# A four-layer transformer trunk on one core: the tiles and copies of two attentions in another order

## The reference, cut to what matters

```python
def _mha(x, y, wq, wk, wv, li1_w, li1_b, ..., causal):
    xn = _ln(x, lnx_g, lnx_b)
    yn = _ln(y, lny_g, lny_b)
    q = jnp.einsum('bsc,hcd->bhsd', xn, wq)
    k = jnp.einsum('btc,hcd->bhtd', yn, wk)
    v = jnp.einsum('btc,hcd->bhtd', yn, wv)
    a = jax.nn.softmax(jnp.einsum('bhsd,bhtd->bhst', q, k) * D ** (-0.5), axis=-1)
    if causal:
        a = a * mask                      # after the softmax
    o = jnp.einsum('bhst,bhtd->bhsd', a, v)
    o = o.transpose(0, 2, 1, 3).reshape(x.shape[0], x.shape[1], H * D)
    x_out = x + o @ li1_w + li1_b
    ...
x = _ln(xx, ln1_g, ln1_b)
x = x + _mha(x, x, a1_..., causal=True)    # stage L2a1, 128 keys
x = _ln(x, ln2_g, ln2_b)
return x + _mha(x, ee, a2_..., causal=False)   # stage L2a2, 77 keys of the context
```

## Time and profile before

| | |
|---|---|
| median of 3 runs | 1132.48 us |
| lowest and highest | 1130.48 and 1135.90 us |
| the profiled execution | 1135.39 us |
| its span in the trace | 1133.7 us |
| L2a1 in the trace, from its first table load to its last product | 450.1 to 602.3 us |
| L2a2, the same | 631.6 to 764.1 us |

### The profile page before, as it was taken

The page is one execution under the profiler, slowest core; times in us unless marked ns, Lnnn a source line. Parts: engine busy times, 40 slices in busy tenths (PEclk is TensorE's granted clock), DMA queues, the critical chain, the costliest instruction groups (busy, mean ns, idle before and its releaser), DMA issues. The chain is left out here.

```text
span 1133.7 us, 35842 instructions
## 1 busy us (share of the span) xinstructions
PE 870.2 (77%) x14276; PEld 670.3 (59%) x14340; DVE 831.6 (73%) x2248; ACT 701.4 (62%) x1469; POOL 570.7 (50%) x600
## 2 busy tenths in 40 slices
PE   3788678779998565688888688989569966876776
PEld 2466477547677354255675466775468944655675
DVE  4888767788877897688877777757566767887555
ACT  4887467766665665676558666657156755974444
POOL 3575735665557345264363422222542656867375
PEclk9898779989999977799999899988679977996588
DMA  5363143411110100100001000000033230111120
GB/s 138 91 136 49 47 123 104 101 41 38 30 30 21 45 12 30 46 22 13 4 4 48 2 3 4 4 4 1 29 96 107 76 80 24 56 34 53 48 73 21
DMA packets 63584, 53.48 MB, mean 47 GB/s; under 512 B 14480, under 2 KB 51859, under 8 KB 63293
## 3 DMA queue, kind: packets, MB, share of 16 engines
q1 hardware_dynamic: 57196, 41.95, 13.9%
q0 software_dynamic: 4544, 8.43, 2.5%
q10 hardware_dynamic: 1683, 0.81, 0.3%
HBM read 34.53 MB, written 17.24 MB: 46 GB/s over the span
## 5 line engine op out<-in xcount | busy, mean ns | idle before, releaser
L1501 ACT ACTIVATE area<-psum 128x512 bf16<-128x512 f32 (+2 forms) x164 | 85.7, 538 | 114.3 <-PE psum L786 54.1
L2137 DVE TENSOR_TENSOR area<-psum,area 128x512 bf16<-128x512 f32 (+3 forms) x156 | 92.6, 618 | 36.6 <-ACT area L1501 34.9
L2843 DVE TENSOR_TENSOR area<-area 128x512 bf16<-128x512 f32 x106 | 74.4, 706 | 44.1 <-ACT area L2023 30.6
L1683 ACT ACTIVATE area<-psum 77x1024 f32<-77x1024 f32 (+1 forms) x96 | 92.7, 1016 | 19.7 <-PE psum L939 13.1
L1410 PE MATMUL psum<-xT_hi,moe 128*128 128x128 bf16 x848 | 100.3, 230 | 3.9 <-issue 2.0
L2960 POOL TENSOR_TENSOR moe<-stage,moe 128x512 bf16<-128x512 f32 x47 | 54.1, 1157 | 78.3 <-ACT moe L1496 78.2
L1428 PE MATMUL psum<-moe,area 128*128 x424 | 87.3, 286 | 0.2 <-DVE area L2843 0.2
L1410 PE MATMUL psum<-xT_lo,moe 128*128 128x128 bf16 x424 | 86.2, 231 | 0.0
L3088 POOL TENSOR_TENSOR area<-area 128x640 bf16<-128x640 f32 x64 | 79.1, 1257 | 10.6 <-ACT area L1842 10.6
L2953 POOL TENSOR_SCALAR rstd<-moments 128x4 f32<-128x4 f32 (+1 forms) x49 | 16.7, 340 | 133.8 <-DVE moments L2122 133.2
L1410 PEld LDWEIGHTS psum<-xT_hi,moe 128*128 x848 | 77.7, 104 | 8.5 <-issue 5.8
(11 more groups left out here) (288 smaller groups left out, 3036.7 us busy)
## 6 DMA issues: line engine op xcount, KB each, us to landing
stage<-in_w_L0m SPq DMA_DIRECT2D x16, 256.0 KB, 2.9
area<-sorted_in SPq DMA_DIRECT2D x16, 256.0 KB, 3.5
sorted_out<-area SPq DMA_DIRECT2D x16, 256.0 KB, 2.6
stage<-in_w_L2m SPq DMA_DIRECT2D x16, 256.0 KB, 2.8
stage<-in_w_L3m SPq DMA_DIRECT2D x16, 256.0 KB, 2.8
sorted_in<-area SPq DMA_DIRECT2D x2, 1472.0 KB, 7.9
stage<-in_w_L2a SPq DMA_DIRECT2D x8, 320.0 KB, 3.3
wide_rows<-area SPq DMA_DIRECT2D x2, 960.0 KB, 10.6
```

The source lines that it names most:

```text
L1501: ins = act.activation(out, bank, ACT.Copy)
L1683: act.activation(A.PF[n % 4][0:A.L, :].rearrange("p (k n) -> p k n", k=2), K.ST[0:A.L, 2 * half:2 * half + 2, :], ACT.Exp, scale=A.scale). ...
L2137: ins = dve.tensor_tensor(out, bank, high, ALU.subtract)
L2843: dve.tensor_tensor(R.HL[u], R.HF[u], upper(R.HF[u]), ALU.subtract).then_inc(K.tile_split, tiles.one())
```

## The change

The one loop is replaced by three, one for each kind of attention. That of L1x holds its old order. In L2a1 and L2a2 the same instructions stand in another order on PE, ACT, DVE and POOL; none is added or taken away, and the buffers, the ring and the transfers stay.

```diff
@@ tensor_program, attention (the loop printed above) @@
-    for b in range(B + 4):
-        ahead = b // GB + 1
...
+    def masked_slot(b):
+        ahead = b // GB + 1
+        if 0 <= b - 1 < B:
+            values(b - 1)
+        if 0 <= b - 2 < B:
+            key_scores(b - 2)
+        if b < B:
+            row_maxima(b, (0, 1))
+        if 0 <= b - 1 < B:
+            turn_maxima(b - 1)
+        if 0 <= b - 3 < B:
+            sums(b - 3)
+        if ahead < NG and b % GB == 3:
+            project(ahead, *A.jobs[0])
+            project(ahead, *A.jobs[3])
+        if ahead < NG and b % GB == 1:
+            project(ahead, *A.jobs[1])
+        if b == B + 2:
+            tokens_turned_for(A.next, 0)
+        if ahead < NG and b % GB == 2:
+            project(ahead, *A.jobs[4])
+        if ahead < NG and b % GB == 3:
+            project(ahead, *A.jobs[6])
+        if 0 <= b - 3 < B:
+            turned(b - 3)
+        if b >= 4:
+            out_project(b - 4)
+        if ahead < NG and b % GB == 1:
+            keys_turned(ahead)
+        if ahead < NG and b % GB == 0:
+            tokens_turned_for(A, ahead)
+        if b < B:
+            row_maxima(b, (2, 3))
+        if ahead < NG and b % GB == 2:
+            project(ahead, *A.jobs[2])
+        if 0 <= b - 3 < B:
+            spread(b - 3)
+        if ahead < NG and b % GB == 2:
+            project(ahead, *A.jobs[5])
+        if ahead < NG and b % GB == 3:
+            project(ahead, *A.jobs[7])
...
+    def context_slot(b):
...
+            sums(b - 3)
+        if 0 <= b - 1 < B:
+            turn_maxima(b - 1)
+        if ahead < NG and b % GB == 3:
+            project(ahead, *A.jobs[3])
+        if ahead < NG and b % GB == 2:
+            project(ahead, *A.jobs[1])
+            project(ahead, *A.jobs[4])
+            project(ahead, *A.jobs[6])
+            project(ahead, *A.jobs[0])
+        if 0 <= b - 3 < B:
+            turned(b - 3)
+        if b == B + 2:
+            tokens_turned_for(A.next, 0)
+        if b >= 4:
+            out_project(b - 4)
+        if b < B:
+            row_maxima(b, (2, 3))
+        if 0 <= b - 3 < B:
+            spread(b - 3)
+        if ahead < NG and b % GB == 2:
+            project(ahead, *A.jobs[5])
+            project(ahead, *A.jobs[2])
+        if ahead < NG and b % GB == 3:
+            project(ahead, *A.jobs[7])
+        if ahead < NG and b % GB == 0:
+            tokens_turned_for(A, ahead)
...
@@ scalar_program, attention @@
+    def masked_slot(b):
+        ahead = b // GB + 1
+        if ahead < NG and b % GB == 2:
+            keys_turned(ahead)
+        if ahead < NG and b % GB == 1:
+            group_turned(ahead)
+        if 0 <= b - 1 < B:
+            values(b - 1)
+        if 0 <= b - 2 < B:
+            exponentials(b - 2, 0)
+        if 0 <= b - 1 < B:
+            turn_maxima(b - 1)
+        if ahead < NG and b % GB == 0:
+            normed(name, A.residual, ahead, A.last_turn)
+        if ahead < NG and b % GB == 3:
+            project(ahead, *A.jobs[0])
+        if ahead < NG and b % GB == 1:
+            project(ahead, *A.jobs[1])
+        if ahead < NG and b % GB == 2:
+            project(ahead, *A.jobs[4])
+        if ahead < NG and b % GB == 3:
+            project(ahead, *A.jobs[3])
+            project(ahead, *A.jobs[6])
+        if 0 <= b - 3 < B:
+            turned(b - 3)
+        if 0 <= b - 2 < B:
+            exponentials(b - 2, 1)
+        if ahead < NG and b % GB == 3:
+            project(ahead, *A.jobs[7])
+        if b == B + 1:
+            for g in range(2):
+                normed(A.next.name, A.next.source, g, behind=(name, A.last_turn, g + 2))
+        if ahead < NG and b % GB == 2:
+            project(ahead, *A.jobs[2])
+            project(ahead, *A.jobs[5])
+        if b == B + 2:
+            layer_tokens(A.next, 0, A)
+        for n in K.loads_of(name, b):
+            split_weights(n, lent)
+        if ahead + 1 < NG and b % GB == 1:
+            prepared(A, ahead + 1)
...
@@ vector_program, attention @@
+    def masked_slot(b):
...
+        if ahead + 1 < NG and b % GB == 3:
+            g_stats(ahead + 1)
...
+        if b == B - 3:
+            first_stats()
+        if ahead < NG and b % GB == 3:
+            project(ahead, *A.jobs[6])
+        if b >= 4:
+            out_project(b - 4)
...
@@ gpsimd_program, attention @@
+    def masked_slot(b):
+        ahead = b // GB + 1
+        if b >= 4:
+            outputs_lo(b - 4)
+        if ahead + 1 < NG and b % GB == 3:
+            rstd(slice(0, 128), group(ahead + 1))
+        if ahead + 1 < NG and b % GB == 0:
+            prepare(A, 0, ahead + 1)
+        if ahead + 1 < NG and b % GB == 2:
+            prepare(A, 2, ahead + 1)
+            add_prepared(A, ahead + 1)
+        if 0 <= b - 2 < B:
+            mask(b - 2, 0)
+        if b == B - 3:
+            for g in range(2):
+                rstd(slice(0, 128), group(g))
+        if 0 <= b - 2 < B:
+            mask(b - 2, 1)
+        for n in K.loads_of(A.name, b):
+            split_weights(n)
...
+    def context_slot(b):
+        ahead = b // GB + 1
+        if ahead + 1 < NG and b % GB == 1:
+            prepare(A, 0, ahead + 1)
+        if b >= 4:
+            outputs_lo(b - 4)
...
```

More of the change, by code:

```diff
@@ L1058, in attention @@
                 turn_maxima(b - 1)
-            for kind, tile in A.jobs_at(b, late=False):
-                project(ahead, kind, tile)
+            if ahead < NG and b % GB == 3:
[5 more added lines that the diff above has]
+                project(ahead, *A.jobs[0])
             if 0 <= b - 3 < B:
-                (turned if A.upright else outputs)(b - 3)
-            if A.upright and b >= 4:
+                turned(b - 3)
+            if b == B + 2:
+                tokens_turned_for(A.next, 0)
+            if b >= 4:
                 out_project(b - 4)
@@ L1757, in attention @@
+        slot = folded_slot if A.folded else masked_slot if A.keys_from_x else context_slot
+        for b in range(B + 4):
+            slot(b)
         end()
@@ L2361, in attention @@
                 g_stats(ahead + 1)
-            if A.upright and 0 <= b - 3 < B:
-                sums(b - 3)
-            for kind, tile in A.jobs_at(b, late=False):
-                project(ahead, kind, tile)
-            if not A.upright and 0 <= b - 3 < B:
-                outputs(b - 3)
-            if A.upright and b >= 4:
+            if ahead < NG and b % GB == 1:
+                project(ahead, *A.jobs[0])
+                project(ahead, *A.jobs[1])
+            if ahead < NG and b % GB == 2:
+                project(ahead, *A.jobs[3])
+                project(ahead, *A.jobs[4])
@@ new lines, in folded_slot @@
+            if ahead < NG and b % GB == 3:
+                project(ahead, *A.jobs[6])
+            if 0 <= b - 3 < B:
+                outputs(b - 3)
+            if b < B:
+                row_maxima(b, (2, 3))
+            if b >= 4:
+                turn_outputs(b - 4)
+            if ahead < NG and b % GB == 1:
+                project(ahead, *A.jobs[2])
+            if ahead < NG and b % GB == 2:
+                project(ahead, *A.jobs[5])
+            if ahead < NG and b % GB == 3:
+                project(ahead, *A.jobs[7])
@@ L2373, in attention @@
                 row_maxima(b, (2, 3))
-            if A.upright and 0 <= b - 3 < B:
+            if ahead < NG and b % GB == 2:
+                project(ahead, *A.jobs[2])
+                project(ahead, *A.jobs[5])
+            if 0 <= b - 3 < B:
                 turned(b - 3)
-            if not A.upright and b >= 4:
-                turn_outputs(b - 4)
-            for kind, tile in A.jobs_at(b, late=True):
-                project(ahead, kind, tile)
-            if A.folded and b == 1:
-                fold_lo("o")
@@ L2391, in attention @@
             if b == B + 2:
                 layer_tokens(A.next, 0)
+            if ahead < NG and b % GB == 2:
+                project(ahead, *A.jobs[5])
+            if b == B - 3:
+                first_stats()
+            if ahead < NG and b % GB == 2:
+                project(ahead, *A.jobs[2])
+            if b == B - 2:
+                for g in range(2):
+                    shift_of(g, number["next", g])
+            if ahead < NG and b % GB == 3:
+                project(ahead, *A.jobs[7])
```

241 lines of the change are left out of this document (172 added, 69 removed).

## The result

| | before | changed |
|---|---|---|
| median of 11 runs of each, same chip | 1135.39 us | 1128.01 us |
| lowest and highest | 1130.48, 1141.36 | 1121.74, 1133.85 |
| ratio, 95% interval | | 0.9923 [0.9897, 0.9948] |
| the profiled execution, its span | 1135.39, 1133.7 | 1133.85, 1132.0 |

The change makes the kernel faster by 0.77%; of 1132.48 us that is 8.7 (5.9 to 11.7). The first three runs of before are the 1132.48 shown ahead.

A forecast was written before the change was run, and what follows sets the result against it. PE was taken to bound both stages, DVE close behind in L2a1, leaving PE's waits to win. L2a1 -6.7 and L2a2 -2.0 sum to -8.7 us, from 1132.48 to 1123.8, predicted as 1124; range 1118 to 1131.5.

The forecast's parts named there:

- The lock on L2288: L2a1: POOL's masks hold DVE's L2288 at 0.97 us for 0.30; apart, the 0.47 before the maxima goes.
- Slots without tiles: L2a1, slots 12 to 16: 5.75, 7.2, 5.75, 5.75 and 4.6, together 29.05 us for 31.17, -2.1.
- The wait in slot 13: L2a1: statistics behind the sums; `out_project`'s bank is emptied at 6.4, the values wait, the slot takes 7.2 us.
- Slots 4 to 11: L2a1: slots 4 to 7 take 33.4 us for 35.61, -2.2; slots 8 to 11 take 30.5 for 32.92, -2.4.
- The wait for ACT's token copy in slot 5: L2a1: `prepared` (1.64 us) stands in front of the token copy on ACT, and PE waits some 0.7 for it.
- The end of L2a1: Second exponential 1.5 us later and token tile before the last outputs: last `out_project` at 11.2 instead of 9.8, +1.4.
- The start of L2a2: Slots 1 to 3: query tiles lose their wait on fresh tokens; -2.5 us, between 0 and -4.
- The rows of six tiles: L2a2, slots 6 and 10: six tiles through four banks, stops of 0.65, 0.55 and 0.15; 9.7 and 9.4 us.
- rival B: PE's small stops in the six-tile rows of slots 2, 6 and 10 lower the clock: +9, 1132.8 us; chance 0.08.
- A: The waits only move, to ACT's token copy in slots 4, 5, 8 and 9: 4.5 of 8.7 goes, 1128.3; chance 0.22.
- C: The second exponential becomes PE's bound, some 16 slots each 0.9 us longer: +5.7, 1138.2; chance 0.07.

The follow-up runs named there:

- context alone: New order in L2a2 only, L2a1 keeping the old loop: 1136.26 us, ratio 0.9995 to the kernel before.
- masked alone: Also called experiment 1: new order in L2a1 only, L2a2 keeping the old loop; 1132.57 us, ratio 0.9965 to the kernel before.
- experiment 8: Changed kernel with DVE's next-stage statistics in slot 13 of L2a2 placed behind the sums, ahead of `out_project`: 1127.82 us, ratio 0.9898 to the kernel before.
- experiment 3: Kernel before with one ACT edit in L2a1: a batch's second exponential behind the outputs' copy. 1132.56 us, ratio 0.9964.
- 4: Kernel before with one POOL edit in L2a1: each batch's second mask made a slot later, ahead of its masks. 1147.28 us, ratio 1.008.
- 5: Changed kernel with both exponentials of a batch together again on ACT in L2a1: one execution, 1127.1 us, L2a1 145.93.
- experiment 10: Changed kernel with stage ends mended, early statistics in L2a2 and `prepared` behind the key tokens' copy: 1120.38 us, ratio 0.9871 to the kernel before.
- experiment 7: Changed kernel with next stage's token tile behind the last outputs on PE, and L2a1's last two exponentials together: one execution, 1126.4 us.
- 6: Changed kernel with L2a1's tiles and token tiles in their old places, exponential still late: one execution, 1132.09 us, L2a1 146.67.
- 9: Changed kernel with ACT's `prepared` in L2a1 a slot later, behind the key tokens' copy: one execution, 1129.11 us, L2a1 144.00.

## Why the prediction was right, and where not

Forecast were 1124 us and -8.7; the ratio gives -8.7, with 8.7 of 1132.48. That is closer than the terms deserve; some of it is luck, as the errors below have both signs. Executions of the same code in a stage differ by one to three microseconds, so I take the means over the executions that have a stage's code in common. L2a1 unchanged: 151.96 and 152.75 (context alone), mean 152.36; changed: 146.31, 146.38 (masked alone), 144.64 (experiment 8), mean 145.78: **-6.6**, predicted -6.7. L2a2 unchanged, in four executions (132.23, 134.11, 131.66, 134.69): 133.17; changed, in five (131.33, 130.60, 131.96, 130.24, 129.60): 130.75: **-2.4**, predicted -2.0. Such means still hold the clock's scatter: in slot 14 it fell in all of the four and in three of the five.

*The lock on L2288.* Right, and tested by 3 and 4. The Trainium skill (SBUF — State Buffer, "SBUF: two separate sides") has the exclusive lock; the trace agrees, and puts its price here at 6.0 us of DVE (11.0 to 5.0 for 16) and 0.48 to 0.65 of PE in each of slots 8 to 13 and 15 (experiment 3 against before).

*Slots without tiles.* 5.65, 7.16, 5.67, 5.65 for 5.75, 7.2, 5.75, 5.75 predicted. Of what is won here, 1.6 us are slots 13 and 14, and they come from the early statistics with POOL's order, not from the exponential: experiment 3, without them, leaves slot 14 at 8.26. Slot 16 was put at 4.6 and takes 5.43 here, but 4.63 to 4.65 in four other executions with the same order there: scatter. The wait in slot 13 is the predicted one (timeline of PE):

```profile
570.90 0.39 PE L786 MATMUL psum<-w_a,yT_hi 128*128 128x512 bf16 x1 [1.47 <-DVE area L2501]
```

*Slots 4 to 11.* Predicted 7.5, 8.75, 7.9, 9.25 and 6.9, 7.15, 7.7, 8.75; measured 7.33, 8.68, 7.92, 9.46 and 6.70, 7.45, 7.91, 9.08. The times are right to 0.35 a slot. The attribution is right in part: I gave the late exponential the leading part, and by 3 and 5 it has that in slots 8 to 11 (2.09 alone, 0.66 without it), while in slots 4 to 7 the rest of the change has it (1.04 and 3.24). Working out only the final order by hand hides that, since it never asks what either edit does without the other. The wait for ACT's token copy in slot 5 was put at 0.7 and is 1.65, and the slot is right all the same (8.68 for 8.75): two errors that cancel. `prepared` in front of the copy is as predicted; no such wait stands in front of the values of slot 10, where one was forecast. The changed kernel, timelines of PE and ACT:

```profile
509.58 0.39 PE L786 MATMUL psum<-w_a,yT_hi 128*128 128x512 bf16 x1 [1.65 <-ACT xT L1711]
```

```profile
506.31 1.02 ACT L1767 ACTIVATE area<-psum 128x1024 f32<-128x1024 f32 x1
507.22 1.64 ACT L1618 ACTIVATE area<-x,shift,rstd 128x128 f32<-128x128 f32 x4
508.75 0.77 ACT L1711 ACTIVATE xT<-psum,cols 128x512 f32<-128x512 f32 x1
```

*The start of L2a1.* Left out of the sum; it gives -1.45. All executions with the new places take 24.0 to 24.6 there, all with the old ones 25.8 to 26.4. So the tiles' places are the cause; what in them, no run took apart.

*The end of L2a1.* +1.4 predicted, +2.09 measured. Both parts named are on the page, the token tile waiting for `normed` and POOL's `outputs_lo` (timeline of PE, for the earlier trace rows):

```profile
594.91 0.63 PE L793 MATMUL psum<-wide,xn 128*128 128x128 f32 x4 [0.54 <-ACT xn L1609]
...
600.33 0.83 PE L786 MATMUL psum<-w_a,area 128*128 128x128 bf16 x12 [2.38 <-POOL area L3310]
```

*The start of L2a2.* Put at -2.5 together with slots 2 and 3, and -0.25 in the pair of profiles. Most of that miss is the clock, ahead of everything that the change moves. From the table load to the first maxima (L896) both programs have the same order; the kernel before takes 8.66 us there at a granted clock of 1.00, the changed one 10.75 at 0.68, and the best version (experiment 10), with the order of the changed one, 8.67 at 1.00. Timelines of PE in these three (table loads at 631.61, 630.53 and 622.14):

```profile
640.27 0.35 PE L896 MATMUL psum<-area 32*128 32x77 bf16 x16 [1.50 <-DVE area L2137]
```

```profile
641.28 0.35 PE L896 MATMUL psum<-area 32*128 32x77 bf16 x16 [1.51 <-DVE area L2314]
```

```profile
630.81 0.35 PE L896 MATMUL psum<-area 32*128 32x77 bf16 x16 [1.50 <-DVE area L2316]
```

From these maxima to slot 2 the four executions with the old order take 9.87 or 9.88 us and the nine with the new order 7.01 or 7.02: -2.86. The wait on fresh tokens (0.89 us in the kernel before) did go, and PE waits 1.36 for DVE's maxima instead. Slots 2 and 3 then lose 0.5 (14.20 for 13.68). With the stretch ahead at equal clock, start and slots 2 and 3 give -2.3 together, so the step holds; the profiled pair alone would have called it false. Timeline of PE in the changed kernel, then its window of slot 2:

```profile
646.92 0.44 PE L896 MATMUL psum<-area 32*128 32x77 bf16 x8 [1.36 <-DVE negm L2455]
```

```profile
648.30:656.30 8.00, 7.32 (x104) 4.11 (x103) 4.77 (x10) 5.20 (x10) 2.53 (x2) 0.72 0.00 0
```

Slot 2 takes 7.99 us, where it took 6.47 before at 0.89: the first three of its six tiles are made at the low clock, and I had costed them at the full-clock spacing.

*The rows of six tiles.* Slots 6 and 10 take 9.06 and 8.77, predicted 9.7 and 9.4: of the three stops that I counted only the one in front of a key tile, for the bank of the sums, is there, with 0.32 and 0.33 for 0.65; those of 0.55 and 0.15 are not. This is the term that was sized most wrongly: slots 4 to 11 were put at +0.2 together and give -1.33. (In four other executions slot 6 takes 9.60 or 9.61, with a stop of 0.45 in the group of the sums for which the trace names no engine.) The clock stays full in slot 6 (window):

```profile
674.94:684.00 9.06, 8.62 (x212) 5.67 (x212) 7.25 (x15) 6.02 (x12) 3.95 (x4) 1.00 0.02 4
```

So rival B did not come true in slots 6 and 10; in slot 2 the clock is low for the first 4.5 us, but it had fallen before the slot began. By the Trainium skill (TensorE: Matmul & The Clock Gate, "A second HAM failure mode: psum-queue depth-cycling") rows of products through cycled banks would be the place; in slots 6 and 10 the trace shows stops of 0.33 us at most and no fall. Falls inside the loops came behind waits of 0.91 to 2.04 us instead, and not in every execution.

*Rivals A and C.* A in part: the waits for ACT's token copy exist (2.8 us in all); the forecast had counted them in, not all at their size. C did not happen: `key_scores` waits for the exponential once in the loop, by 0.24 at the start of slot 17.

**What stays open:** why the clock falls behind a wait of 1.25 or 1.65 us in one execution and not in another; whether the new order makes a low clock at the start of L2a2 likelier (eight of nine executions with it had one, and two of four with the old order); and the difference of some microseconds ahead of L2a1 between executions.

## What to carry to other kernels

When two edits remove the same wait, work out or run each alone before crediting either: here one exponential moved on one engine gives 4.05 us, the rest of the change without it 6.03, and both 5.65. Before you call a term of a forecast wrong, compare stretches at the same granted clock: here 2.1 us of it hid a gain of 2.86. An instruction of DVE that took two or three times its usual length and ended just behind one of POOL's was a lock here, and what feeds POOL cured it; delaying POOL itself moved the lock to another instruction of DVE and put other work behind it. Look at a stage's two ends by themselves: an order that is better in the steady slots cost 2.09 us in the tail.

## What the runs showed of the hardware

The clock can fall to half behind one wait, and whether it does varies between executions of the same code. Behind 1.65 us in slot 5 of L2a1 it held in the changed kernel and fell in experiment 1, 1.6 us dearer over slots 5 and 6; it held behind 1.88 in the same place in experiment 8 and fell behind 2.04 in experiment 7. Behind 1.25 us in slot 14 of L2a2 it fell in both first profiles and in experiments 1 to 5, and held in experiments 6, 7 and 9, where that slot takes 7.74 us, not 9.38: 1.64; slot 15 takes 5.88 to 6.15 for 6.25 to 6.46. The changed kernel's window behind that wait:

```profile
735.50:741.50 6.00, 6.00 (x134) 4.56 (x135) 2.26 (x7) 1.12 (x2) 1.04 (x1) 0.50 0.03 5
```

At a stage's start it costs more: 10.75 us for 8.66 or 8.67 up to the first maxima of L2a2.

The lock between DVE and POOL goes to whichever instruction of DVE with two operands in SBUF stands beside the mask: L2288 took 0.97 us for 0.30, and with the mask a slot later L2241 took 1.35 for 0.69.
